# One core, eight images: row gathers without accumulation, row statistics moved to GpSimd, and sorting, scatters and logits spread over more steps

## The chip, the cores and the metric

The kernel runs on one core of one Trainium2 chip. The metric is the device time of one execution in microseconds (us). Engines: PE is TensorE (matrix products; PEld its weight loads), DVE is VectorE, ACT is ScalarE, POOL is GpSimd, SP is SyncE, which here only issues transfers. Each engine runs its own list of instructions in order and waits on semaphores where it needs another engine's result.

## What is computed

Eight images of 48x48 positions with 128 channels each. Per image:

```
x = x + ss2d(group_norm(x))            # 32 groups; 256 inner channels, 3x3 depthwise convolution,
                                       # scan over L = 2304 positions with 16 states:
                                       #   h = exp(dt*A)*h + dB*x ;  y = sum(h*C) + Dskip*x
t = tokens(x)                          # 2304 rows of 128
t = t + attention(layer_norm(t))       # 8 heads of 16, linear attention: softmax(q), softmax(k),
                                       # context = k'v, out = q context, projection, layer_norm
u = layer_norm(t)                      # routing: logits = u Wg (8 experts), best two, softmax of the two
t = t + sum over the two experts of weight * W2 (silu(W1 u) * (W3 u + b3))
```

The first layer norm of the tokens is followed at once by the one that the attention applies, so a row needs three statistics (a mean and a variance over 128 channels): of the tokens (two norms folded into one), of the attention's output, and of the sum.

## The kernel before

A row tile is 128 rows, so an image has 18 of them (NT). The scan takes an image in 6 chunks (c) of 384 positions; a chunk has 32 steps (n), one for each block of 8 of the 256 inner channels with 16 states on 128 partitions. A pass has 192 steps (k = 32c + n). All engines walk the same steps, and the images are pipelined over passes: in a pass one image is scanned (i), the image before it goes through attention, routing and scatter (j), the one before that through its experts (p), the one before that has its results gathered and summed (q), and the next image is loaded, normalised and convolved (nx). L420 and the lines behind it write the passes out: eight with a scan, of which images 3 to 6 are a loop; then a last pass without a scan (T_END = 362 steps), in which image 7 is routed, image 6's and image 7's experts run, and the last results are gathered.

In each step of the scan PE spreads the inputs (L768) into one of three PSUM buffers, DVE multiplies (inflow, L1407) and scans (L1420), ACT makes the decay three steps ahead (L1041), POOL multiplies the state by C (prod, L627, eight buffers) and PE folds that (L831). Around it:

- **Row statistics** (DVE): `spread_of` (L1497 to L1504), eight operations on 128x18 numbers, each waiting for the one before by a semaphore (`tie`); ACT takes the root (L1161, L1163); `offsets` (L1507). At steps 22, 24, 26 (T_STAT, with L1594 to L1599), 82 and 84 (T_STAT2), 98 and 100 (T_STAT3).
- **Routing**: the logits (PE, L896, 18 products, six a step from step 110), best two (DVE, from 113), the rank by a product at 118, sorting into expert tiles at 119 to 123.
- **Scatter** (POOL, L681): 36 indirect DMAs that write rows of 129 numbers to `rows_in` in DRAM, one at each step from 125 to 160; after 18 of them the weight column is replaced (L678).
- **Experts**: 45 tiles of 128 rows, some at steps 126 to 191 and the rest at steps 0 to 26 of the pass behind. A tile is loaded, transposed (PE L910, ACT L1209), multiplied up (PE L921 and L933, ACT L1212 and L1221, DVE L1661), its two halves multiplied on POOL (`hidden`, L697), multiplied down (PE L940), and stored to `rows_out`.
- **Gather** (POOL, L709): 36 indirect DMAs per image with compute_op=ADD; SP first loads a row tile of the sum so far into one of six buffers (acc_in, L573), each gather adds 128 rows of 128 numbers to it, the second one 4 steps behind the first, which it waits for; SP stores the tile as output (L577). Steps 34 to 110 of a pass.
- **The next image**: x_in has three buffers of a sixth of an image; its loads are issued at steps 114 to 116, and from step 128 on behind the transposes (PE L738) that free a buffer. Transposes at 125 to 135, statistics of each sixth (L1366), group norm (L1371 to L1378 at step 138, L1382 to L1385 at 140, L1389 at 141) and the normalising at step 145.
- **Products with weights on POOL**: L663, L668 (attention output, steps 86 to 94), L656 (62 to 64), L633 and L640 once a chunk.

Of the kernel before, what the change touches and what calls it, by code (L numbers as in the profile page):

```python
# [47 lines left out]
XR, XI = 2, 3  # L48
WA, WB = 3, 5
UIN, UOUT, UT, HID = 7, 3, 3, 2  # L50
GA = 6
# [12 lines left out]
T_XLOAD = tuple(NB * TURN - 14 + g if g < XI else T_TURN[g - XI] + 3 for g in range(NC))  # L64
# [5 lines left out]
T_STAT, T_BACK, T_NORM = 22, 25, 29  # L70
# [17 lines left out]
T_END = T_GATHER[-1] + STORE + 1 + SC - SOONEST  # L88
DVE_POST = 53
# [3 lines left out]
LAG = 2  # L93
TILE = tuple(T_TILE + (T_LAST - T_TILE) * u // (NU + LAG - 1) for u in range(NU + LAG))

# [54 lines left out]
def build(nc, a):  # L150

    with ExitStack() as ctx:
# [3 lines left out]
        def psum(name):  # L156
# [27 lines left out]
        x_in = sb("x_in", [P, XI, TT, D])  # L184
# [27 lines left out]
        acc_in = sb("acc_in", [P, GA, D])  # L212
# [3 lines left out]
        gdev = sb("gdev", [P, 2 * NC])  # L216
# [13 lines left out]
                             for k in range(3))  # L230
        tile_expert, expert_of = sb("tile_expert", [P, NU]), sb("expert_of", [P, 2, NU], I32)
# [6 lines left out]
        acc = q_tok  # L238
# [116 lines left out]
        s_x = [Sem(f"s_x{b}", NC // XI, 16) for b in range(XI)]  # L355
# [4 lines left out]
        dve_gn = Sem("dve_gn", NC + 9)  # L360
# [21 lines left out]
        s_weight, s_rows = Sem("s_weight", 1), Sem("s_rows", 1)  # L382
        s_accout = Sem("s_accout", 1, 16)
        s_top, s_topexp, s_sorted = Sem("s_top", 1), Sem("s_topexp", 1), Sem("s_sorted", 2)
        dve_post = Sem("dve_post", DVE_POST)
# [9 lines left out]
        s_gather = [Sem(f"s_gather{b}", NT // GA * TOP, 16) for b in range(GA)]  # L395
        s_accin = [Sem(f"s_accin{b}", NT // GA, 16) for b in range(GA)]
        s_out = [Sem(f"s_out{b}", NT // GA, 16, first=16) for b in range(GA)]

# [34 lines left out]
        def _(sp):  # L433
# [69 lines left out]
            def load_x(w, g):  # L503
                if w.nx is None:
                    return
                if g >= XI:
                    sp.wait_ge(*full(w.nx, f"xT{g - XI}"))
                elif w.i is not None:
                    sp.wait_ge(*full(w.i, f"xT{g + NC - XI}"))
                apart()  # L510
                sp.dma_start(x_in[:, g % XI], x_chunk(w.nx, g)).then_inc(s_x[g % XI].sem, 16)
# [38 lines left out]
            def experts(m, t):  # L550
# [15 lines left out]
                for x in range(NT):  # L566
                    if t == T_GATHER[x] - 3:
                        if x == 0:
                            due(sp, s_accout, m, 1)
                            apart()  # L570
                        due(sp, s_out[x % GA], m, x // GA)
                        apart()
                        sp.dma_start(acc_in[:, x % GA], image_rows(acc_dram, m)[:, D * x:D * x + D]).then_inc(s_accin[x % GA].sem, 16)  # L573
                    if t == T_GATHER[x] + STORE:
                        due(sp, s_gather[x % GA], m, TOP * (x // GA + 1))
                        apart()
                        sp.dma_start(a["out"][bass.ds(image_of(m), 1)][:, P * x:P * x + P, :].rearrange("o p d -> p (o d)"),  # L577
                                     acc_in[:, x % GA]).then_inc(s_out[x % GA].sem, 16)

            def run(w, first, last):  # L580
                for k in range(first, last):
# [11 lines left out]
                    for g in range(NC):  # L593
                        if k == T_XLOAD[g]:
                            load_x(w, g)
# [13 lines left out]
            for b in range(GA):  # L609
                sp.wait_ge(s_out[b].sem, s_out[b].at(B, 0))  # L610

        @block.gpsimd
        def _(pool):
# [28 lines left out]
            def attention(m, t):  # L642
                if m is None:
                    return
                for h in range(2):
# [23 lines left out]
                k = t - T_SCATTER  # L669
                if 0 <= k < NSC:  # L670
# [13 lines left out]
            def experts(m, t):  # L684
                if m is None:
                    return
                if t == T_ROWS:
                    for b in range(GA):
                        due(pool, s_gather[b], m, s_gather[b].per)
                    pool.sem_inc(s_rows.sem, 1)  # L690
# [7 lines left out]
                for n in range(TOP):  # L698
                    if t - SECOND * n in T_GATHER:
                        x = T_GATHER.index(t - SECOND * n)  # L700
                        if n == 0:
                            if x == 0:
                                for b in range(UOUT):
                                    due(pool, s_ostore[b], m, s_ostore[b].per)
                            due(pool, s_accin[x % GA], m, x // GA + 1)
                        else:
                            due(pool, s_gather[x % GA], m, TOP * (x // GA) + 1)
                        pool.sem_inc(s_sp.sem, 1)
                        pool.indirect_dma_start(acc_in[:, x % GA], None, rows_out,  # L709
                                                bass.IndirectOffsetOnAxis(ap=row_of[:, parity(m), n * NT + x:n * NT + x + 1], axis=0),  # L710
                                                compute_op=ALU.add).then_inc(s_gather[x % GA].sem, 16)

            def run(w, first, last):
                for k in range(first, last):
# [8 lines left out]
                    attention(w.j, k)  # L723
# [282 lines left out]
        def _(act):  # L1006
# [225 lines left out]
            def attention(m, t):  # L1232
                if m is None:
                    return
                if t == T_STAT + 1:
                    root(m, 1, r1[:, :])
# [497 lines left out]
```

## Time and profile before

| | us |
|---|---|
| time, median of 3 runs | 4248.45 (4237.47 to 4254.57) |
| the profiled execution | 4259.8, of which the span is 4257.7 |
| PE busy | 3281.3 (77%) |
| DVE busy | 3117.9 (73%) |
| POOL busy | 2942.6 (69%) |
| ACT busy | 2565.0 (60%) |
| mean granted clock of PE | 0.89 of full speed |

By the start of their first scan the passes take 361, 401, 444, 489, 491, 502, 489 and 469 us (images 0 to 7), behind a start of 86 us, and the last pass 526 us. Times are read from one profiled execution. The busy share is an average over stages that have different limits, so the stretches of one pass are what is read below; a stretch is a chunk of 32 steps or a part of it. A row of the windows gives from:to and its length, then the busy time and number of instructions of PE, PEld, DVE, ACT and POOL in that order, then the granted clock of PE, the DMA share and GB/s; the stretch of chunk 2 begins at step 62. A bracket behind an operation is the idle time of its engine before it and what ended it.

### The profile page before, as it was taken

What the parts mean: (1) busy time and instruction counts of PE and PEld (TensorE: products, weight loads), DVE (VectorE), ACT (ScalarE), POOL (GpSimd) and SP (SyncE); (2) the same over time, 40 slices, a digit from 0 to 9 for tenths busy, and PEclk for the clock granted to TensorE, in tenths of its full rate; (3) what the DMA queues carried; (4) which work ended last, traced back from release to release, by engine and by line L of the source; (5) the groups of instructions that cost most, each with busy time, mean ns of one, the idle gap of its engine ahead of it and who ended that gap; (6) DMA issues with size and microseconds to landing.
All of it is one profiled execution on the core that took longest, in us unless ns stands there. A gap on an engine that the chain in (4) does not pass through costs nothing.

```text
span 4257.7 us, 69497 instructions
## 1 busy us (share of the span) xinstructions
PE 3281.3 (77%) x17432; PEld 1995.0 (47%) x17432; DVE 3117.9 (73%) x5570; ACT 2565.0 (60%) x6151; POOL 2942.6 (69%) x2703
## 2 busy tenths in 40 slices
PE   5687887787798868987788877888688877778381
PEld 2233343343465535653465434655356534567271
DVE  3699998899867987789776988779877897723110
ACT  3465665476567656775576755676467765666151
POOL 1465675857676968679685886669686796757665
PEclk9798997898899979998899978999799988999695
DMA  4865555555787658966687676876588666868493
GB/s 103 194 154 134 145 127 124 135 144 139 189 218 201 144 142 218 235 164 145 169 226 193 146 164 177 219 195 143 140 228 233 154 149 178 221 184 231 117 257 76
DMA packets 464099, 730.07 MB, mean 171 GB/s; under 512 B 58505, under 2 KB 362194, under 8 KB 461522
## 3 DMA queue, kind: packets, MB, share of 16 engines
q1 hardware_dynamic: 313938, 484.13, 46.5%
q10 hardware_dynamic: 99072, 203.47, 16.1%
q0 software_dynamic: 50688, 37.93, 5.2%
q8 instruction: 152, 2.49, 0.3%
q14 instruction: 249, 2.04, 0.2%
HBM read 596.93 MB, written 100.07 MB: 164 GB/s over the span
## 4 chain that ended last, share of the span: by engine, by line
PE 34%; issue 17%; DVE 16%; POOL 14%; ACT 11%; DMA 4%; ACTq 2%; SPq 1%; DVEq 0%; POOLq 0%
PE ps_conv L754 7%; DVE state L1420 6%; PE ps_main L817 5%; POOL prod L627 5%; PE ps_h L921 3%; PE ps_y L831 3%; POOL rows_in L681 3%; PE ps_g L940 3%; DVE ps_x L1407 3%; PE ps_x L768 3%; PE ps_g L933 3%; POOL acc_in L709 3%; ACT dt_rep L1041 2%; ACT big_u L1169 1%; DVE silu L1661 1%
## 5 line engine op out<-in xcount | busy, mean ns | idle before, releaser
L627 POOL TENSOR_TENSOR prod<-state,c_rep 128x384 f32<-128x384 f32 x1536 | 1659.0, 1120 | 937.9 <-DVE state L1420 912.9
L1420 DVE TENSOR_TENSOR_SCAN state<-dt_rep,carry,ps_x 128x384 f32<-128x384 f32 x1280 | 1284.0, 1003 | 0.0
L1407 DVE TENSOR_TENSOR ps_x<-ps_x,db_rep 128x384 f32<-128x384 f32 x1536 | 854.0, 556 | 397.7 <-PE ps_x L768 360.0
L1041 ACT ACTIVATE dt_rep<-dt_rep,vecs 128x384 f32<-128x384 f32 x1536 | 913.3, 611 | 182.0 <-DMA dt_rep<-dt_dram 104.1
L768 PE MATMUL ps_x<-x_stack,copy 96*128 96x384 bf16 x1536 | 546.9, 357 | 392.3 <-DVE state L1420 386.4
L754 PE MATMUL ps_conv<-gx,w_conv 128*128 128x384 f32 x1728 | 695.9, 522 | 8.7 <-DVE parts L1437 6.0
L768 PEld LDWEIGHTS ps_x<-x_stack,copy 96*128 96x128 bf16 x1536 | 154.5, 101 | 882.1 <-DVE state L1420 635.9
L709 POOL DMA_INDIRECT acc_in<-rows_out,row_of x288 | 452.6, 1572 | 97.8 <-issue 46.3
L921 PE MATMUL ps_h<-u_t,w_up 128*128 128x128 f32 x2064 | 325.1, 296 | 188.4 <-DVE silu L1661 170.5
L697 POOL TENSOR_TENSOR hidden<-g_sb,silu 128x384 f32<-128x384 f32 x344 | 363.7, 1060 | 104.4 <-ACT u_out L1227 98.9
L754 PEld LDWEIGHTS ps_conv<-gx,w_conv 128*128 128x128 f32 x1728 | 320.9, 203 | 227.6 <-issue 119.7
L1221 ACT ACTIVATE g_sb<-ps_g,w_down 128x128 f32<-128x128 f32 x1032 | 304.1, 368 | 199.6 <-PE ps_g L940 164.6
L1661 DVE SCALAR_TENSOR_TENSOR silu<-silu,ps_h 128x384 f32<-128x384 f32 x344 | 185.8, 540 | 300.4 <-ACT silu L1212 193.6
L921 PEld LDWEIGHTS ps_h<-u_t,w_up 128*128 128x128 f32 x2064 | 275.5, 200 | 276.2 <-issue 165.9
L831 PE MATMUL ps_y<-prod,fold 128*32 128x384 f32 x3072 | 361.2, 545 | 22.9 <-POOL prod L627 22.9
L681 POOL DMA_INDIRECT rows_in<-big_u,row_of x288 | 291.1, 1011 | 83.8 <-issue 76.4
L940 PE MATMUL ps_g<-w_down,hidden 128*128 128x128 f32 x2064 | 299.4, 282 | 34.1 <-POOL hidden L697 25.4
L933 PE MATMUL ps_g<-u_t,w_up 128*128 128x128 f32 x2064 | 309.4, 288 | 11.9 <-ACT u_out L1227 8.1
L933 PEld LDWEIGHTS ps_g<-u_t,w_up 128*128 128x128 f32 x2064 | 289.3, 202 | 51.4 <-issue 25.9
L940 PEld LDWEIGHTS ps_g<-w_down,hidden 128*128 128x128 f32 x2064 | 268.2, 198 | 41.7 <-POOL hidden L697 29.0
L1420 DVE TENSOR_TENSOR_SCAN state<-dt_rep,ps_x 128x384 f32<-128x384 f32 x256 | 241.4, 943 | 16.4 <-ACT carry L1050 16.4
L1212 ACT ACTIVATE silu<-ps_h 128x384 f32<-128x384 f32 x344 | 168.1, 489 | 48.6 <-POOL hidden L697 38.6
(245 smaller groups left out, 4928.9 us busy)
## 6 DMA issues: line engine op xcount, KB each, us to landing
dt_rep<-dt_dram SPq DMA_DIRECT2D x384, 768.0 KB
w_up<-in_w_exp ACTq DMA_DIRECT2D x344, 384.0 KB
w_down<-in_w_exp ACTq DMA_DIRECT2D x344, 193.5 KB
x_stack<-parts SPq DMA_DIRECT2D x576, 48.0 KB
u_in<-rows_in SPq DMA_DIRECT2D x344, 64.5 KB
rows_out<-u_out SPq DMA_DIRECT2D x344, 64.0 KB
dt_dram<-dt SPq DMA_DIRECT2D x192, 96.0 KB
x_in<-in_x SPq DMA_DIRECT2D x48, 192.0 KB
```

The lines of the kernel that those rows point to most:

```text
L627: pool.tensor_tensor(prod[:, k % HS, :], state[:, k % HS, :], c_rep[:, c % 2, :], ALU.mult).then_inc(s_prod.sem, 1)
L681: pool.indirect_dma_start(rows_in, bass.IndirectOffsetOnAxis(ap=row_of[:, parity(m), k:k + 1], axis=0), big_u[:, k % NT, :], None).then_in ...
L709: pool.indirect_dma_start(acc_in[:, x % GA], None, rows_out, bass.IndirectOffsetOnAxis(ap=row_of[:, parity(m), n * NT + x:n * NT + x + 1], ...
L754: ins = pe.matmul(aux(use)[:, 0:T], w_conv[:, tap, P * hf:P * hf + P], gx[:, ROWS * c + dy:ROWS * c + dy + ROWS, dx:dx + W], start=tap == ...
L768: pe.matmul(ps_x[k % XB][:, 0:T], copy[:, b, :], x_stack[:, c % 2, HV * q + hf, :], start=True, stop=True).then_inc(s_xrep.sem, 1)
L831: ins = pe.matmul(ps_y[32 * q:32 * q + 32, 0:T], fold[:, b, :], prod[:, (QD * m + q) % HS, :], start=b == 0, stop=b == 3)
L921: ins = pe.matmul(aux(name)[:, P * k:P * k + P], w_up[:, u % WA, P * k:P * k + P], u_t[:, u % UT, :], start=True, stop=True)
L933: ins = pe.matmul(aux(name)[:, P * k:P * k + P], w_up[:, u % WA, F + P * k:F + P * k + P], u_t[:, u % UT, :], start=True, stop=True)
L940: ins = pe.matmul(aux(name)[:, F:F + P], hidden[:, v % HID, P * k:P * k + P], w_down[:, v % WB, P * k:P * k + P], start=k == 0, stop=k == ...
L1041: act.activation(dt_rep[:, g % XS, q, :], dt_rep[:, g % XS, q, :], ACT.Exp, scale=decay_rate).then_inc(s_decay.sem, 1)
L1407: dve.tensor_tensor(x_n, x_n, db_rep[:, c % 2, :], ALU.mult).then_inc(s_inflow.sem, 1)
L1420: dve.tensor_tensor_scan(state[:, k % HS, :], dt_rep[:, g % XS, q, :], ps_x[k % XB][:, 0:T], init, ALU.mult, ALU.add).then_inc(s_state.sem, 1)
```

## The change

In neutral words, part by part:

1. **Gather**: 36 plain gathers (no compute_op) into `got` (two pairs of row tiles, two rows each), at T_GATHER = 34 + 23x//5 (steps 34 to 112), the second two steps behind the first, and none waits for another. POOL adds: at T_SUM (43, 52, 62, 71, 80, 89, 98, 108, 117) a 128x256 addition of the two gathers, a step later a 128x256 addition to acc_in, which SP loads and stores by pairs.
2. **Row statistics**: `spread_of` and `offsets` run on POOL (26 small operations an image, 19 of which are followed by a wait for themselves, `settle`), at steps 23, 25, 27 / 82, 84 / 97, 99. ACT's root takes the scale and the small constant.
3. **Group norm**: one bn_aggr in place of L1371 to L1378, at n = 9 in place of 10; three of the small operations go to ACT.
4. **Next image**: x_in lies where the sum (`acc`, q_tok) lay; six loads issued at steps 112 to 117, and the first transpose waits for all.
5. **Logits and sorting**: six steps of three products (108 to 113) in place of three of six; best two from 114, rank at 121 and copied by ACT, sorting at 122 to 130.
6. **Scatter**: steps 132 to 190, spread (132 + 58k//35); for the last image 132 + k. T_END is 368.

The core of the diff:

```diff
-T_XLOAD = tuple(NB * TURN - 14 + g if g < XI else T_TURN[g - XI] + 3 for g in range(NC))
+T_XLOAD = NB * TURN - 16
-T_STAT, T_BACK, T_NORM = 22, 25, 29
+T_STAT, T_BACK, T_NORM = 23, 25, 29
-T_AGAIN, T_STAT2, T_NORM2, T_STAT3, T_NORM3, T_UT, T_LOGIT = 81, 82, 85, 98, 101, 103, 110
+T_AGAIN, T_STAT2, T_NORM2, T_STAT3, T_NORM3, T_UT, T_LOGIT = 81, 82, 85, 97, 100, 102, 108
-T_TOP, T_RANK, T_SORT, T_SCATTER = 113, 118, 119, 125
+T_TOP, T_RANK, T_SORT = 114, 121, 122
-T_GATHER = tuple(2 * SC + k for k in (34, 37, 40, 43, 46, 49, 52, 66, 69, 72, 75, 78, 81, 84, 97, 100, 103, 106))
-T_ROWS, SECOND, STORE = 2 * SC + 114, 4, 9
+T_GATHER = tuple(2 * SC + 34 + 23 * x // 5 for x in range(NT))
+SECOND = 2
+T_SUM = tuple(T_GATHER[2 * g + 1] + SECOND + 3 for g in range(NG))
+STORE = 4
+T_SCATTER = tuple(132 + 58 * k // (NSC - 1) for k in range(NSC))
+T_SCATTER_LAST = tuple(132 + k for k in range(NSC))
...
-        acc = q_tok
+        acc = x_in = q_tok
...
+            def settle(m, ins):
+                count[0] += 1
+                ins.then_inc(pool_post.sem, 1)
+                due(pool, pool_post, m, count[0])
+
+            def spread_of(m, src):
+                settle(m, pool.tensor_tensor(mv[:, :, 0], src[:, :, 1], src[:, :, 4], ALU.subtract))
+                settle(m, pool.tensor_tensor(mv[:, :, 1], src[:, :, 2], src[:, :, 5], ALU.add))
+                settle(m, pool.tensor_tensor(mv[:, :, 0], mv[:, :, 0], mv[:, :, 0], ALU.mult))
+                pool.sem_inc(s_sp.sem, 1)
+                settle(m, pool.tensor_scalar(mv[:, :, 0], mv[:, :, 0], D / 4.0, None, ALU.mult))
+                pool.tensor_tensor(mv[:, :, 1], mv[:, :, 0], mv[:, :, 1], ALU.add).then_inc(s_var.sem, 1)
+
+            def offsets(m, src):
+                settle(m, pool.tensor_tensor(mv[:, :, 0], src[:, :, 1], src[:, :, 4], ALU.add))
+                pool.sem_inc(s_sp.sem, 1)
+                settle(m, pool.tensor_scalar(mv[:, :, 0], mv[:, :, 0], -0.5, None, ALU.mult))
+                pool.tensor_tensor(nb[:, :], mv[:, :, 0], r1[:, :], ALU.mult).then_inc(s_coef.sem, 1)
...
+                if t in (T_STAT2, T_STAT3):
+                    due(pool, s_stats, m, 1 if t == T_STAT2 else 2)
+                    spread_of(m, st)
+                if t in (T_STAT2 + 2, T_STAT3 + 2):
+                    due(pool, s_root, m, 3 if t == T_STAT2 + 2 else 4)
+                    offsets(m, st)
...
-                        pool.indirect_dma_start(acc_in[:, x % GA], None, rows_out,
-                                                bass.IndirectOffsetOnAxis(ap=row_of[:, parity(m), n * NT + x:n * NT + x + 1], axis=0),
-                                                compute_op=ALU.add).then_inc(s_gather[x % GA].sem, 16)
+                        pool.indirect_dma_start(got[:, g % RG, n, x % 2, :], None, rows_out,
+                                                bass.IndirectOffsetOnAxis(ap=row_of[:, parity(m), n * NT + x:n * NT + x + 1], axis=0)
+                                                ).then_inc(s_gather[g % RG].sem, 16)
+                for g in range(NG):
+                    first = got[:, g % RG, 0]
+                    if t == T_SUM[g]:
+                        due(pool, s_gather[g % RG], m, 2 * TOP * (g // RG + 1))
+                        pool.tensor_tensor(first, first, got[:, g % RG, 1], ALU.add).then_inc(s_sum.sem, 1)
+                    if t == T_SUM[g] + 1:
+                        due(pool, s_sum, m, 2 * g + 1)
+                        due(pool, s_accin[g % RG], m, g // RG + 1)
+                        pool.tensor_tensor(acc_in[:, g % RG], acc_in[:, g % RG], first, ALU.add).then_inc(s_sum.sem, 1)
...
-                due(pe, s_x[g % XI], i, g // XI + 1)
+                due(pe, s_x, i, NC)
...
+                if n == 9:
+                    dve.sem_inc(s_sp.sem, 1)
+                    dve.bn_aggr(gmv[:, 0:2], gst[:, :, :].rearrange("p g k -> p (g k)")).then_inc(s_gn.sem, 1)
```

## Rows read from the trace of the kernel before

**Rows 1.** The page's first part: busy time of each engine, share of the span

```profile
PE 3281.3 (77%) x17432; PEld 1995.0 (47%) x17432; DVE 3117.9 (73%) x5570; ACT 2565.0 (60%) x6151; POOL 2942.6 (69%) x2703
```

**Rows 2.** Windows of image 4 (chunks 0, 2, 4, 5): us, busy by engine, clock, DMA

```profile
1781.30:1860.40 79.10, 68.22 (x407) 44.48 (x406) 61.24 (x106) 61.07 (x152) 46.81 (x47) 0.96 0.77 203
...
1929.00:2004.80 75.80, 55.84 (x258) 28.01 (x251) 71.62 (x128) 43.26 (x97) 72.11 (x63) 0.84 0.63 142
...
2092.00:2187.00 95.00, 79.26 (x482) 56.06 (x481) 68.85 (x115) 63.00 (x164) 79.30 (x79) 0.94 0.81 221
2187.00:2272.40 85.40, 75.78 (x482) 53.02 (x481) 60.94 (x96) 58.07 (x156) 57.06 (x57) 0.98 0.86 229
```

**Rows 3.** Timeline of DVE, image 4, step 22: start, duration, operation

```profile
1840.46 0.17 DVE L1497 TENSOR_TENSOR mv<-st_t 128x18 f32<-128x18 f32 x1
...
1843.62 0.57 DVE L1407 TENSOR_TENSOR ps_x<-ps_x,db_rep 128x384 f32<-128x384 f32 x1
```

**Rows 4.** Timeline of all engines, image 4, around step 82

```profile
1966.25 3.43 DVE L1497 TENSOR_TENSOR mv<-st 128x18 f32<-128x18 f32 x1
...
1970.15 3.22 DVE L1500 SCALAR_TENSOR_TENSOR mv<-mv 128x18 f32<-128x18 f32 x1
1970.79 2.54 POOL L627 TENSOR_TENSOR prod<-state,c_rep 128x384 f32<-128x384 f32 x2
...
1976.25 0.57 DVE L1407 TENSOR_TENSOR ps_x<-ps_x,db_rep 128x384 f32<-128x384 f32 x1
1976.36 0.22 ACT L1161 ACTIVATE r<-r 128x18 f32<-128x18 f32 x1 [12.58 <-DVE r L1504]
```

**Rows 5.** POOL by line, image 4, steps 62 to 95: busy, mean ns, idle before

```profile
L627 POOL TENSOR_TENSOR prod<-state,c_rep 128x384 f32<-128x384 f32 x33 | 43.8, 1441 | 2.9 <-DVE state L1420 2.9
L709 POOL DMA_INDIRECT acc_in<-rows_out,row_of x14 | 22.0, 1572 | 2.2 <-issue 1.9
```

**Rows 6.** Durations by line, whole trace: ns least/median/most, first and last start

```profile
L681 POOL DMA_INDIRECT rows_in<-big_u,row_of x288: 959/998/1719, 718.4 to 4021.8; - x144
L709 POOL DMA_INDIRECT acc_in<-rows_out,row_of x288: 1542/1571/1624, 1378.6 to 4252.3; - x144
L678 POOL COPY big_u<-gw x8: 205/210/218, 762.9 to 3981.9; 128x18 f32<-128x18 f32 x8
L633 POOL TENSOR_TENSOR dt<-dt,dt_tmp x48: 1792/1818/2412, 71.6 to 3605.7; 128x768 f32<-128x768 f32 x48
```

**Rows 7.** Timeline of POOL, image 4, the scatter behind L678

```profile
2144.54 1.71 POOL L681 DMA_INDIRECT rows_in<-big_u,row_of  x1 [0.89 <-POOL big_u L678]
```

**Rows 8.** Timeline of DVE, image 4, step 98

```profile
2010.17 0.17 DVE L1497 TENSOR_TENSOR mv<-st 128x18 f32<-128x18 f32 x1
...
2013.77 0.57 DVE L1407 TENSOR_TENSOR ps_x<-ps_x,db_rep 128x384 f32<-128x384 f32 x1
```

**Rows 9.** PE by line, image 4, steps 110 to 114: busy, mean ns, idle before

```profile
L896 PE MATMUL ps_g<-w_gate,qv 128*128 128x8 f32 x36 | 6.3, 308 | 1.4 <-ACT qv L1032 1.4
```

**Rows 10.** Timeline of PE, image 4, step 135

```profile
2115.79 0.52 PE L738 MATMUL ps_conv<-eye,x_in 128*128 128x128 f32 x3 [3.43 <-DMA x_in<-in_x]
```

**Rows 11.** Timeline of DVE, image 4, steps 138 to 141

```profile
2121.72 0.14 DVE L1371 TENSOR_REDUCE gmv<-gst 128x1 f32<-128x12 f32 x1
...
2124.78 0.56 DVE L1661 SCALAR_TENSOR_TENSOR silu<-silu,ps_h 128x384 f32<-128x384 f32 x1
...
2135.91 0.16 DVE L1389 TENSOR_SCALAR gmv<-ps_conv 128x1 f32<-128x1 f32 x1 [2.65 <-PE ps_conv L745]
```

**Rows 12.** Waits in chunk 4 of image 7 (89.4 us): total, times, longest

```profile
ACT silu L1212 <- POOL hidden L697: 11.8, 5, 5.6
```

**Rows 13.** Timeline of POOL, the last gathers

```profile
4175.37 1.58 POOL L709 DMA_INDIRECT acc_in<-rows_out,row_of  x1 [5.11 <-DMA acc_in<-acc_dram]
4177.25 1.56 POOL L709 DMA_INDIRECT acc_in<-rows_out,row_of  x1 [0.30 <-issue]
...
4252.27 1.56 POOL L709 DMA_INDIRECT acc_in<-rows_out,row_of  x1 [0.70 <-issue]
```

More of the change, by code:

```diff
@@ L352, in build @@
         s_sp = Sem("s_sp", 0)
-        s_x = [Sem(f"s_x{b}", NC // XI, 16) for b in range(XI)]
+        s_x = Sem("s_x", NC, 16)
         s_res = [Sem(f"s_res{b}", NC // XR, 16) for b in range(XR)]
@@ L505, in load_x @@
                     return
-                if g >= XI:
-                    sp.wait_ge(*full(w.nx, f"xT{g - XI}"))
+                if g:
+                    pass
+                elif w.j is not None:
+                    due(sp, s_accout, w.j, 1)
+                    apart()
+                    due(sp, s_xn, w.j, 3 * NC)
                 elif w.i is not None:
-                    sp.wait_ge(*full(w.i, f"xT{g + NC - XI}"))
+                    sp.wait_ge(*full(w.i, f"xT{NC - 1}"))
                 apart()
-                sp.dma_start(x_in[:, g % XI], x_chunk(w.nx, g)).then_inc(s_x[g % XI].sem, 16)
+                sp.dma_start(x_in[:, TT * g:TT * g + TT], x_chunk(w.nx, g)).then_inc(s_x.sem, 16)
             def load_residual(w, c):
@@ L592, in run @@
                         store_t1(w, c)
-                    for g in range(NC):
-                        if k == T_XLOAD[g]:
-                            load_x(w, g)
+                    if 0 <= k - T_XLOAD < NC:
+                        load_x(w, k - T_XLOAD)
                     for m, t in w.experts(k):
@@ L608, in _ @@
             passes(sp, run)
-            for b in range(GA):
+            for b in range(RG):
                 sp.wait_ge(s_out[b].sem, s_out[b].at(B, 0))
@@ L686, in experts @@
                     return
[L687 to L690, printed above, removed]
                 u = tile_of.get(t - 3)
@@ L894, in logits @@
                         pe.wait_ge(*read(m, x))
-                for k in range(6 * part, 6 * part + 6):
+                for k in range(TT * part, TT * part + TT):
                     ins = pe.matmul(o[:, NE * k:NE * k + NE], turned[:, P * k:P * k + P], w_gate[:, :], start=True, stop=True)
-                if part == 2:
+                if part == NC - 1:
                     ins.then_inc(fills("logit", m), 1)
@@ L1552, in count_experts @@
             def count_experts(m):
-                dve.wait_ge(*full(m, "rank"))
-                tie(m, dve.tensor_copy(tally[:, 0, :], aux("rank", m)[:, NE * NT:NE * NT + NE]))
-                tie(m, dve.tensor_scalar(tally[:, 3, :], tally[:, 0, :], 1.0 / P, None, ALU.mult))
+                dve.wait_ge(*read(m, "rank"))
+                tie(m, dve.tensor_scalar(tally[:, 3, :], counts[:, NE * NT:NE * NT + NE], 1.0 / P, None, ALU.mult))
                 tie(m, dve.tensor_tensor(picked[:, :, :], tally[:, 3, :].unsqueeze(2).broadcast_to([P, NE, NT]),
```

242 lines of the change are left out of this document (111 added, 131 removed).

## The prediction

> **What bounds the kernel now.** I read first the page's busy times [rows 1]: PE 77%, DVE 73%, POOL 69%, and nobody is full. Such a page says that the loss is in the coupling, so the next view is the windows of one pass, chunk by chunk [rows 2], of image 4, since images 3 to 6 run the same loop. There each chunk has another limit. Chunk 0 takes 79.1 us with PE busy for 68.2 and POOL for 46.8: PE is near its end, POOL has 32 us free. From step 62 to 95 (75.8 us) it is POOL with 72.1, and DVE shows 71.6. Chunk 4 takes 95.0 with PE and POOL both at 79.3; chunk 5 85.4 with PE at 75.8 and POOL at 57.1. Then I read the timelines where steps are long. The scan needs PE's spread, DVE and POOL in turn with only a few buffers between, so whatever holds DVE for some us in one step is mostly lost to the pass, even where DVE has idle time a few steps later.
>
> Four such places stand out. At step 22 the eight row statistics hold DVE from 1840.46 to 1843.62, 3.2 us [rows 3]. At step 82 the same eight hold it from 1966.25 to 1976.25, 10 us [rows 4]: an operation on 18 numbers that takes 0.17 alone lasts 3.4 or 3.2, and the 3.22 us one ends with POOL's two multiplications that run beside it. ACT waits 12.58 us for the result. At step 98 they take 3.6 us [rows 8]. And at step 138 the group norm's eight take 3.1 [rows 11], a few steps behind PE's wait of 3.43 for x_in [rows 10].
>
> **The change part by part.** The sum is made against the profiled 4259.8; it is 11.4 above the median of 4248.45, and I subtract the difference from the median.
>
> *Statistics.* DVE loses 30 small operations an image, POOL gets 26. What one costs on POOL: its 128x18 copy takes 0.21 [rows 6]. Its wait for itself has no row; the scatter behind the copy, which waits in that way, starts 0.89 us later [rows 7], where a DMA without such a wait starts 0.30 behind the one before it [rows 13], so at most 0.6. From the other side, eight operations linked in the same way on DVE take 3.1 us with all waits [rows 11], under 0.4 each. I take 0.32 for operation and wait, nearer to the second row since both are chains of computation. Steps 23 to 27 on POOL: 10 x 0.32 = 3 us, hidden in its 32 free us. DVE's 3.2 us at step 22 go, and five more operations at 24 and 26 of at least 0.17 each: 4 us, all counted (bounds -1, if PE with 68.2 of 79.1 is late next, to -5). At step 98 it is 3.6, counted as 3.3, in a chunk where POOL has room.
>
> At step 82 POOL has none, and this is the place where I don't count what DVE loses. POOL's account for steps 62 to 95 [rows 5, 6]: 14 accumulating gathers of 1.57 with 0.16 of issue, 24.2 us, go. 15 plain ones come. No plain gather is in the trace; the nearest is the scatter, also an indirect DMA of 128 rows without an accumulation, 1.00 us; with 0.16 that makes 17.4. Bounds are 1.00 and 1.57, and I take the lower. Four sum pairs lie here. From 1.82 for 768 columns and 0.21 for 18 a 256-column addition is 0.21 + 238 x 2.14 ns = 0.72; with two waits a pair is 1.56, four are 6.2. The statistic at 82 and 84 is eight operations, 2.6. Together -24.2 + 17.4 + 6.2 + 2.6 = +2.0. So the stretch stays as long as it is, though DVE is rid of 10 us: DVE waits for POOL where it now waits inside its own operations. Bounds -7 (sums and statistics find gaps) to +12 (each own wait 0.6, and the sums wait for late gathers).
>
> A rule of the Trainium skill speaks against this move: "GPSIMD Engine Reference", section 4.1, keeps elementwise work of two inputs on VectorE, with GpSimd about half as fast. By it an operation would be about 0.36 us and the sum here some 1 us per statistic later; the copy's 0.21 against 0.17 on DVE doesn't show a factor of two at 18 columns [rows 3, 6].
>
> *Logits.* PE's products of 8 columns take 6.3 us in three steps (the row counts 36) and hold the spread of steps 112 and 113 behind them [rows 9]; three a step instead of six is counted as -2. Sorting keeps its DVE work, in nine steps for five: 0, and at worst +2 where a step with sorting meets a full one of POOL. Chunk 3 with step 98: -5.3, say -5.5.
>
> *Next image.* The loads are issued at 112 to 117 rather than up to step 132, so the wait of 3.43 [rows 10] goes: -3 (the six in a burst delay other loads at worst by 2). They need the sum's last reader, long done at step 112. Behind them on SP stand the decay loads and the tiles' row loads, both some steps early.
>
> *Group norm.* bn_aggr for eight operations: 3.1 less one of at most 0.6, since 384 columns take 0.57 [rows 3, 11], -2.5. Of the small ones at 140 and 141 DVE keeps two; its wait of 2.65 for PE there goes, as ACT takes that step, and three operations of 0.2 to 0.4: -3.5. Bounds -2 to -6.
>
> *Scatters.* They leave steps 125 to 131 and lie at 132 to 190, 17 in chunk 4 and 19 in chunk 5 (35 and 1 before). An issue costs 1.00 + 0.25. Chunk 5's POOL goes from 57.1 to 57.1 + 18 x 1.25 = 79.6 of 85.4. I count +2 there and -0.5 in chunk 4, which with x_in and group norm gives -9.5.
>
> Images 3 to 6: -4 + 0 + 2 - 5.5 - 9.5 + 2 = -15 each, -60 (chunk 1 has none of the edits that count). Image 7 has no next image: -4 + 2 - 5.5 - 3.5 (35 scatters spread where POOL makes ACT wait 11.8 us [rows 12]) = -11. Image 2, with no gathers in its pass, -16.5; image 1, in its short chunks, -13; image 0 has only the group norm, -5; the start -1.5.
>
> *The last pass.* Its end is POOL alone, from 5.11 before 4175.37 to 4257.7, 87.4 us: 36 gathers 1.88 apart and four waits of 5 for acc_dram [rows 13]. After: a pair of tiles is 4 x 1.28 + 1.95 = 7.07, nine are 64, with 7 for the first landing and the last store 71: -16 (bounds 0 at 1.57 a gather, to -20). The two earlier gather phases of this pass and image 7's scatters: -14 (bounds 0 to -25).
>
> Sum: -1.5 - 5 - 13 - 16.5 - 60 - 11 - 30 = -137. 4259.8 - 137 - 11.4 = 4111.
>
> **The rivals.** *A, the plain gather costs 1.57 too* (issue time is per row, not per kind). For it: both move 128 rows. Against: the scatter's 1.00. Then +0.57 x 15 = 8.6 in five passes and 36 x 0.57 = 20.5 in the end: 4111 + 63 = 4174.
>
> *B, PE takes what DVE gives back.* For it: 68.2 of 79.1 and 79.3 of 95.0 [rows 2]. Against: PE waits for DVE's scan in these steps. Chunks 0, 3 and 4 give 3, 4 and 5 less in six passes: +72, 4183.
>
> *C, slower: POOL's statistics hold ACT.* A statistic becomes a chain POOL, ACT, POOL, ACT, in POOL's order behind its multiplications. It decides where POOL lags the scan by more than the three steps by which ACT's decay is early; then ACT, which waits in order, starves the scan. The price is what ACT waits at step 82, 12.58 [rows 4], at the two other places too, in seven passes: 2 x 12.6 x 7 = 176, 4287. Against it: POOL has 32 us free in chunk 0, so it doesn't lag there.
>
> *D, more is gained: POOL yields at step 82.* DVE's 10 us go there whole and the +2 with them, in five passes: 4111 - 60 = 4051. For it: DVE's waits there end with POOL's operations, so it is DVE that yields now. The Trainium skill, "SBUF — State Buffer", section on the two sides, says that DVE and GpSimd hold a shared port pair exclusively for a whole instruction; the 3.22 us ending with POOL's multiplications agrees [rows 4], and by that rule the blocked time leaves with the moved operations.
>
> *E, scatters in chunk 5 make POOL late.* Above 85.4 - 79.6 = 5.8 us of waits POOL becomes the bound and `hidden` comes late, as image 7's chunk 4 shows [rows 12]. Price 18 x 1.25 = 22.5 less the 2 counted, in seven passes: +143, 4254, no change.
>
> **How the numbers follow.** Forecast 4111: 0.42, its own range 4075 to 4150. A 0.12, B 0.12, C 0.10, D 0.15, E 0.09. A measurement of this kernel tells about 0.5% from no change, 21 us, so faster means under 4227: forecast, A, B and D, 0.81; same is E, 0.09; slower C, 0.10. The range leaves out C and E (0.19): from below D, 4020, to above B with its bounds, 4215.
>
> **What would show it.** In the changed kernel's windows: chunk 0 near 75, steps 62 to 95 near 76 with POOL still above 70, chunk 4 near 85, chunk 5 near 87. On the gather's line near 1.00 us; a POOL operation of 18 columns near 0.21 with gaps near 0.1. PE's transposes of x_in without a wait for DMA. The end from the last tile on near 71. Wrong would make it: gathers at 1.57 (A), ACT waiting for POOL's r or nb for over 7 us in chunk 0 or 3 (C), waits for `hidden` over 10 us in chunk 5 (E), or DVE without a wait for POOL at step 82 (D).

## The result: 0.7% faster, a fifth of what was forecast

The changed kernel takes 4227.05 us (median of 18 runs, 4209.72 to 4244.81) against 4254.66 for the kernel before in the same sessions (18 runs): a ratio of 0.9931, 95% interval 0.9916 to 0.9945. It is faster, as forecast, by 28 us and not by 137; the time lies above the range. The profiled execution went from a span of 4257.7 to 4218.1, -39.6, 12 us more than the medians differ by, and the readings below are made against that pair.

| where (profiled spans, us) | forecast | measured |
|---|---|---|
| start | -1.5 | +1.1 |
| image 0 | -5 | -5.8 |
| image 1 | -13 | -13.4 |
| images 2 to 6, five passes | -76.5 | +22.9 |
| image 7 | -11 | -12.6 |
| last pass | -30 | -31.8 |

The miss is in the five passes that have both expert tiles and a next image. For one of them, by stretches of steps (mean of images 2 to 6; the forecast is that for images 3 to 6):

| steps | what the change does there | forecast | measured |
|---|---|---|---|
| 0 to 31 | first statistic | -4 | -2.9 |
| 32 to 61 | gathers, sums | 0 | -0.2 |
| 62 to 96 | gathers, sums, second statistic | +2 | 0.0 |
| 97 to 107 | third statistic | -3.5 | +2.4 |
| 108 to 113 | logits | -2 | -1.6 |
| 114 to 131 | sorting | 0 | +4.1 |
| 132 to 144 | next image, group norm | -9 | -5.1 |
| 145 to 149 | (normalising, no edit counted) | 0 | +5.6 |
| 150 to 164 | scatters | -0.5 | -1.3 |
| 165 | (weight copy, no edit counted) | 0 | +4.7 |
| 166 to 191 | scatters | +2 | -1.0 |
| all | | -15 | +4.6 |

The windows of image 4 in the changed kernel, which answer to [rows 2] (chunk 0, steps 62 to 95, chunks 4 and 5; columns as there):

```profile
1772.40:1850.40 78.00, 68.23 (x406) 44.18 (x405) 56.95 (x93) 58.27 (x148) 49.48 (x58) 0.95 0.79 207
...
1918.30:1995.80 77.50, 54.87 (x260) 26.34 (x252) 62.06 (x120) 43.18 (x97) 71.07 (x79) 0.87 0.57 141
...
2084.10:2181.10 97.00, 79.68 (x474) 55.74 (x475) 71.71 (x111) 61.29 (x160) 66.53 (x65) 0.91 0.75 199
2181.10:2268.40 87.30, 76.02 (x482) 52.69 (x481) 60.94 (x96) 57.50 (x156) 70.55 (x72) 0.98 0.88 235
```

DVE is rid of 4.3 us in chunk 0 and of 9.6 from step 62 to 95, and POOL of 12.8 in chunk 4. Yet chunk 4 is longer (97.0 against 95.0), with DVE 2.9 us busier. Durations of POOL's operations, which answer to [rows 6] (least, median and most in ns):

```profile
L756 POOL DMA_INDIRECT got<-rows_out,row_of x288: 940/987/1052, 1367.4 to 4211.7; - x144
...
L763 POOL TENSOR_TENSOR got<-got x72: 717/730/750, 1389.4 to 4214.3; 128x256 f32<-128x256 f32 x72
...
L663 POOL TENSOR_TENSOR mv<-st x16: 235/244/254, 599.2 to 3889.4; 128x18 f32<-128x18 f32 x16
```

A plain gather takes 0.99 us where an accumulating one took 1.57, an addition of 256 columns 0.73, a small operation 0.24, or 0.35 from its start to that of the next behind its wait, where 0.32 was forecast: the prices were right. The last gathers, which answer to [rows 13]:

```profile
4153.65 0.99 POOL L756 DMA_INDIRECT got<-rows_out,row_of  x1 [4.01 <-DMA rows_out<-u_out]
4154.94 0.94 POOL L756 DMA_INDIRECT got<-rows_out,row_of  x1 [0.30 <-issue]
...
4214.27 0.72 POOL L763 TENSOR_TENSOR got<-got 128x256 f32<-128x256 f32 x1 [1.61 <-DMA got<-rows_out,row_of]
```

From the wait ahead of the first (4149.6) to the end (4218.1) the phase takes 68.5 us, 87.4 before; 71 was forecast.

### The profile page after: what moved, and what is told of

Same layout as the page of the kernel before. It is cut to its first block and busy times, and to the rows that moved or that the text cites. A ratio compares the mean times of both kernels' runs of the same rounds, so it can differ in the third digit from the quotient of the medians.

```text
span 4218.1 us, 69032 instructions
## 1 busy us (share of the span) xinstructions
PE 3292.7 (78%) x17432; PEld 1992.9 (47%) x17432; DVE 3006.8 (71%) x5234; ACT 2556.1 (61%) x6173; POOL 2917.0 (69%) x3055
## 3 DMA queue, kind: packets, MB, share of 16 engines
q10 hardware_dynamic: 99072, 203.47, 16.1%
## 5 line engine op out<-in xcount | busy, mean ns | idle before, releaser
L638 POOL TENSOR_TENSOR prod<-state,c_rep 128x384 f32<-128x384 f32 x1536 | 1530.2, 1002 | 899.3 <-DVE state L1471 867.5
L745 POOL TENSOR_TENSOR hidden<-g_sb,silu 128x384 f32<-128x384 f32 x344 | 343.6, 999 | 115.0 <-ACT u_out L1291 103.4
L756 POOL DMA_INDIRECT got<-rows_out,row_of x288 | 283.9, 986 | 61.9 <-issue 38.7
L996 PEld LDWEIGHTS ps_g<-w_down,hidden 128*128 128x128 f32 x2064 | 268.3, 198 | 41.5 <-POOL hidden L745 31.5
L1273 ACT ACTIVATE u_t<-ps_h 128x128 f32<-128x128 f32 x328 | 89.8, 274 | 195.9 <-PE ps_h L966 179.3
```

The source lines that it names most:

```text
L638: pool.tensor_tensor(prod[:, k % HS, :], state[:, k % HS, :], c_rep[:, c % 2, :], ALU.mult).then_inc(s_prod.sem, 1)
L745: pool.tensor_tensor(hidden[:, u % HID, :], g_sb[:, u % 2, :], silu[:, u % 2, :], ALU.mult).then_inc(s_hidden.sem, 1)
L996: ins = pe.matmul(aux(name)[:, F:F + P], hidden[:, v % HID, P * k:P * k + P], w_down[:, v % WB, P * k:P * k + P], start=k == 0, stop=k == ...
```

## The experiments

Times are medians; each kernel is the changed one with one edit, and "after" is the changed kernel. Five-pass means are of images 3 to 7 unless it is said otherwise. The kernel before took 4250.8 to 4257.9 us by the median beside these runs, so their times can be set against the changed kernel's 4227 to within some 10 us.

**The weight copy.** What was read first, in image 4 of the changed kernel around step 165 (timeline; in brackets the idle time before and what ended it):

```profile
2192.19 0.21 POOL L730 COPY big_u<-gw 128x18 f32<-128x18 f32 x1 [5.64 <-DMA rows_in<-big_u,row_of]
...
2196.23 0.49 ACT L1276 ACTIVATE silu<-ps_h 128x384 f32<-128x384 f32 x1 [4.08 <-POOL hidden L745]
...
2200.32 0.57 DVE L1458 TENSOR_TENSOR ps_x<-ps_x,db_rep 128x384 f32<-128x384 f32 x1 [3.01 <-PE ps_x L824]
```

POOL stands still for 5.64 us until the eighteenth scatter has landed, `hidden` is late, so ACT is late, so the spread. Ahead of the copy stands one operation of 1.00 us behind the scatter's issue (2184.51 to 2185.52). Before the change, in image 4, there were three, and no wait:

```profile
2138.73 1.00 POOL L681 DMA_INDIRECT rows_in<-big_u,row_of  x1 [0.16 <-issue]
2139.77 1.00 POOL L627 TENSOR_TENSOR prod<-state,c_rep 128x384 f32<-128x384 f32 x1
2140.72 1.81 POOL L640 TENSOR_TENSOR y<-y,sz 128x768 f32<-128x768 f32 x1
2142.50 0.99 POOL L697 TENSOR_TENSOR hidden<-g_sb,silu 128x384 f32<-128x384 f32 x1
2143.44 0.21 POOL L678 COPY big_u<-gw 128x18 f32<-128x18 f32 x1
```

```diff
-T_SCATTER = tuple(132 + 58 * k // (NSC - 1) for k in range(NSC))
+T_SCATTER = tuple(132 + 23 * k // (NT - 1) for k in range(NT)) + tuple(163 + 27 * k // (NT - 1) for k in range(NT))
```

> The changed kernel, but the first 18 scatters of an image lie at steps 132 to 155 and the other 18 at 163 to 190, so that the copy of the second weight column, which waits for the first 18 to land, comes eight steps behind the last of them and not one. Theory W (the wait behind the 18th scatter): in the changed kernel GpSimd stands 5.64 us before that copy at step 161, hidden comes late and step 165 lasts 7.5 us in place of 2.8; with the steps between, step 165 falls by about 4.7 us in six passes: 4227 - 28 = 4199 us. Rival E of the prediction (scatters in the last chunk are simply too much for GpSimd): the last chunk still has 18 of them, so it stays at 87 us and the time at 4227.

Measured: 4184.89 us, 0.9815 of the kernel before (0.9775 to 0.9855). Step 165 went from 7.2 to 2.6 us; the copy waits for no DMA anywhere in the trace, here in image 4:

```profile
2184.99 0.22 POOL L730 COPY big_u<-gw 128x18 f32<-128x18 f32 x1
```

The theory held for the step, but only about half of its gain reaches the time: steps 166 to 178 went from 28.9 to 31.4 us in images 2 to 6, and to 31.2 to 31.5 in the three kernels below that have this edit too. In image 3 ACT now waits there 2.7 us for a store of `rows_out`, which it doesn't in the changed kernel; whether waits of this kind make up the whole 2.5 us was not followed. Chunk 5 takes 82.1 us in images 2 to 6, 84.2 after and 81.9 before the change. So rival E of the prediction fell: with 18 scatters the chunk is as long as with one. The gain is nevertheless larger than expected because step 145 fell too, by 3.1 us in images 2 to 6 (5.2 with the steps up to 149), without an edit there; the third run tells why.

**Sorting.**

```diff
                 if t == T_SORT + 1:
                     count_experts(m)
+                    sum_experts(m)
                 if t == T_SORT + 2:
-                    sum_experts(m)
+                    place_experts(m)
+                    route(m, 7)
                 if t == T_SORT + 3:
-                    place_experts(m)
+                    place_rows(m, 0)
+                    place_rows(m, 1)
                 if t == T_SORT + 4:
-                    route(m, 7)
-                if t in (T_SORT + 5, T_SORT + 6):
-                    place_rows(m, t - T_SORT - 5)
-                if t == T_SORT + 7:
                     place_tiles(m, before_m)
-                if t == T_SORT + 8:
                     place_last(m)
```

> The changed kernel, but the sorting operations stand in five steps (122 to 126) and not in nine (122 to 130). Theory P (small VectorE operations stretched by GpSimd's multiplication, which starts anew in each step): VectorE's busy time of steps 114 to 131, 50.2 us in image 4 against 45.7 before the change, comes back to about 46 to 47, 3 to 4 us in each of seven passes: 4227 - 25 = 4202. Rival (the sum of the operations is the same wherever they stand, and TensorE's expert tiles set the pace of steps 126 to 131): no change, 4227.

Measured: 4232.1 us, 0.995 (0.9926 to 0.9975). The windows of steps 114 to 131 in image 4, first after, then this run:

```profile
2043.30:2096.40 53.10, 35.97 (x164) 19.53 (x165) 50.22 (x135) 18.60 (x46) 21.85 (x23) 0.78 0.48 124
```

```profile
2044.30:2098.90 54.60, 36.45 (x161) 19.86 (x162) 47.91 (x135) 18.67 (x46) 22.15 (x23) 0.78 0.48 124
```

DVE's busy time, the third number, fell by 2.3 us: the same operations last longer when they are spread. That POOL's multiplication stretches them was argued, not tried. In images 3 to 7 the time didn't follow (54.0 us, 52.7 after), as the rival says. In image 1, in whose pass there are no expert tiles, it did: 47.8 us, 49.7 after.

**Normalising the next image.** In image 4 of the changed kernel, step 145:

```profile
2133.16 4.58 DVE L1446 TENSOR_SCALAR gx<-gx,gmv 128x2304 f32<-128x2304 f32 x1
2133.62 1.95 POOL L638 TENSOR_TENSOR prod<-state,c_rep 128x384 f32<-128x384 f32 x2
2135.52 0.99 POOL L745 TENSOR_TENSOR hidden<-g_sb,silu 128x384 f32<-128x384 f32 x1
2136.69 1.94 POOL L733 DMA_INDIRECT rows_in<-big_u,row_of  x1 [0.17 <-issue]
```

```diff
+                    act.activation(inner, inner, ACT.Identity, bias=gmv[:, 6:7], scale=rate).then_inc(s_norm.sem, 1)
...
-                    dve.tensor_copy(gmv[:, 4:5], aux("gm")[:, 0:1])
+                    dve.tensor_scalar(gmv[:, 4:5], aux("gm")[:, 0:1], -1.0, None, ALU.mult)
...
-                    dve.tensor_scalar(inner, inner, gmv[:, 5:6], gmv[:, 6:7], ALU.mult, ALU.subtract).then_inc(s_norm.sem, 1)
```

> The changed kernel, but ACT and not VectorE multiplies the 2304 columns of the normalised next image (step 145). Theory P: VectorE's operation takes 4.58 us there because it stands behind two multiplications and a hidden of GpSimd (1.48 before the change, when GpSimd happened to issue a DMA); on ACT it meets no GpSimd operation: step 145 falls by 3 to 4.5 us in images 0 to 6, and steps 147 and 148, which were 2.7 longer at a granted clock of 0.79 (1.00 before), fall by up to 2.7 in images 2 to 6: 4227 - 20 to 4227 - 40, 4197 in the middle. Rival (ACT is late with the decay when it holds 2304 columns for 2 to 3 us): the gain is eaten, 4220 to 4230.

Measured: 4189.04 us, 0.9855 (0.9829 to 0.988). Step 145 fell by 4.5 us in images 2 to 6 and by 2 in images 0 and 1, steps 146 to 149 by about 1, to 15.5 (13.8 before). ACT's operation takes 2.3 us; the only wait for it is PE's of 3.9 us ahead of the first scan. The first run's DVE operation, with its durations over all images, and POOL's beside it in image 4:

```profile
L1446 DVE TENSOR_SCALAR gx<-gx,gmv x8: 1457/1458/1905, 35.2 to 3111.7; 128x2304 f32<-128x2304 f32 x8
...
2132.59 1.94 POOL L733 DMA_INDIRECT rows_in<-big_u,row_of  x1 [0.16 <-issue]
```

Before the change, in image 4, beside the scatter of [rows 7]:

```profile
2144.64 1.48 DVE L1395 TENSOR_SCALAR gx<-gx,gmv 128x2304 f32<-128x2304 f32 x1
```

In both the scatter steps put an indirect DMA on POOL just then (2132.59 to 2134.53 in the first run), and no multiplication until the operation was over. So the edit of the scatter, not one of the normalising, made this step long. The Trainium skill says in "SBUF — State Buffer", in the section on the two sides, that VectorE, in some kinds of operations, and GpSimd share a port pair, which one of them holds for a whole instruction while the other waits. The rows agree on the waiting: the operation ends at 2137.74, and 1.46 before that is 2136.28, near the end of POOL's third operation (2136.51). Why it waits past the ends of the first two is not shown.

**The statistics on DVE again.**

```diff
...
-                if t in (T_STAT2, T_STAT3):
-                    due(pool, s_stats, m, 1 if t == T_STAT2 else 2)
-                    spread_of(m, st)
...
+                if t in (T_STAT2, T_STAT3):
+                    due(dve, s_stats, m, 1 if t == T_STAT2 else 2)
+                    spread_of(m, st)
...
```

(and the first statistic and the offsets likewise)

> The changed kernel, but the three row statistics run on VectorE again, in the changed kernel's form and steps (part 2 undone alone). The prediction's theory (moving them gains 4 us in chunk 0 and 3.3 at the third, and costs 2.6 at the second): 4227 + 5 x 7 = 4260. Theory C' (a chain of GpSimd, ACT, GpSimd, ACT behind GpSimd's other work costs about what VectorE is rid of: step 82 gives 10 us back and steps 71 to 95 take 9 to 10 of it, step 98 gives 3.6 and steps 103 and 105 take 6.5): chunk 0 gets longer by 2, steps 97 to 107 shorter by 3 to 5, step 82 is 10 again: 4220 to 4235.

Measured: 4224.13 us, 0.9922 (0.9898 to 0.9946): the same as after. Steps 22 to 31 are 1.3 us longer, step 82 by 2.0 only, steps 83 to 96 shorter by 2.7, 97 to 107 by 0.9. The move of part 2 to another engine is worth nothing that the times can tell, as the second theory said, but two of its numbers were wrong: step 82 doesn't take 10 us again, and steps 97 to 107 give 0.9 and not 3 to 5. At step 82 there are now five small operations for eight, and POOL no longer has the accumulating gathers beside them; that this is the whole reason was argued, not tried. The 4260 of the first theory left its own 2.6 out: 4 and 3.3 less 2.6 are 4.7 a pass, which makes 4251, and that is missed too.

**Logits and sorting as before the change.**

```diff
-T_AGAIN, T_STAT2, T_NORM2, T_STAT3, T_NORM3, T_UT, T_LOGIT = 81, 82, 85, 97, 100, 102, 108
+T_AGAIN, T_STAT2, T_NORM2, T_STAT3, T_NORM3, T_UT, T_LOGIT = 81, 82, 85, 97, 100, 102, 109
-T_TOP, T_RANK, T_SORT = 114, 121, 122
+T_TOP, T_RANK, T_SORT = 112, 118, 119
```

(and three steps of six products, and the five sorting steps of the second run)

> The changed kernel, but part 5 undone: the logits in three steps of six products (109 to 111), best two from 112, rank at 118, sorting in five steps 119 to 123, as before the change but for one step. Theory T (what costs 4.1 us in steps 114 to 131 of each pass is that sorting now stands in steps 125 to 130, where the first expert tiles run and TensorE needs the step; the second run showed that fewer meetings with GpSimd alone don't give it back): these steps come back from 53.4 to about 49.5 us, 4 us in images 2 to 6 and 1 to 3 in 1 and 7: 4227 - 23 = 4204. The prediction's theory (spread logits gain 2 us, sorting is neutral): 4227 + 14 = 4241.

Measured: 4218.64 us, 0.9912 (0.9884 to 0.9941). Image 4, steps 108 to 113 and 114 to 131:

```profile
2021.30:2042.70 21.40, 19.99 (x70) 13.83 (x71) 12.44 (x36) 9.18 (x22) 14.23 (x14) 0.60 0.77 191
2042.70:2092.50 49.80, 31.73 (x156) 16.68 (x155) 45.12 (x115) 19.46 (x47) 22.25 (x23) 0.83 0.52 132
```

Steps 114 to 131 came back to 49.4 us (52.7 after), as expected; steps 108 to 113 went from 16.7 to 19.9. By the time, the two cancel but for 8 us, less than the medians can tell. So the late place of best two, rank and sorting costs 3 to 4 us a pass in steps 114 to 131, and the spread logits give back about as much (the last section says how far one profile can tell that). The run moves the three together and doesn't show which of them costs.

**The third statistic.** Image 4 of the changed kernel, steps 97 to 105:

```profile
1998.65 0.99 POOL L756 DMA_INDIRECT got<-rows_out,row_of  x1 [0.16 <-issue]
1999.66 1.96 POOL L638 TENSOR_TENSOR prod<-state,c_rep 128x384 f32<-128x384 f32 x2
2001.58 0.24 POOL L663 TENSOR_TENSOR mv<-st 128x18 f32<-128x18 f32 x1
...
2003.23 0.31 ACT L1223 ACTIVATE r<-mv,vecs 128x18 f32<-128x18 f32 x1 [4.55 <-POOL mv L668]
...
2009.01 1.26 ACT L1233 ACTIVATE big_u<-qv,nb,r 128x128 f32<-128x128 f32 x3 [3.28 <-POOL nb L674]
...
2010.42 0.52 PE L931 MATMUL ps_g<-eye,big_u 128*128 128x128 f32 x3 [2.84 <-ACT big_u L1233]
...
2019.92 0.57 DVE L1458 TENSOR_TENSOR ps_x<-ps_x,db_rep 128x384 f32<-128x384 f32 x1 [4.24 <-PE ps_x L824]
```

In steps 97 to 103 POOL starts its multiplication 2 to 7 us behind the start of the step's scan (1 to 2 us in steps 97 to 101 before the change), the statistic waits in its queue, ACT waits for the statistic, PE's transposes for ACT, and DVE's inflow for PE.

```diff
-T_GATHER = tuple(2 * SC + 34 + 23 * x // 5 for x in range(NT))
+T_GATHER = tuple(2 * SC + (34 + 23 * x // 5 if x < 12 else 106 + 3 * (x - 12)) for x in range(NT))
```

> The changed kernel, but the last six row tiles are gathered at steps 106 to 123 in place of 89 to 114, so that GpSimd has no gather and no sum between steps 90 and 105, where the third row statistic stands. Theory C' (GpSimd is up to 6.8 us behind the scan at steps 99 to 102, so ACT waits 4.6 us for the statistic and 3.3 for the offsets, and TensorE's transposes hold the spread): in images 3 to 7 steps 97 to 107 fall by 3 us, to what image 1 shows without gathers, and steps 83 to 96 by 3 to 5 as GpSimd has 6 fewer gathers there: 4227 - 30 = 4197. Rival (the chain itself is too long, one step earlier than before the change, whoever stands ahead of it): steps 97 to 107 stay, 4215 to 4227.

Measured: 4191.01 us, 0.9846 (0.9817 to 0.9874). Steps 83 to 96 went from 39.1 to 34.2 us, 97 to 107 from 26.6 to 22.4, and ACT's waits for POOL's statistic (for r) and offsets (nb) over the second and third statistic of image 4 are these (total, times, longest), first after, then in this run:

```profile
ACT r L1223 <- POOL mv L668: 15.8, 2, 11.3
...
ACT big_u L1233 <- POOL nb L674: 3.3, 1, 3.3
```

```profile
ACT r L1223 <- POOL mv L668: 10.3, 2, 7.8
...
ACT big_u L1233 <- POOL nb L674: 0.4, 1, 0.4
```

The theory held; the chain is not too long by itself. Steps 114 to 131, where some of the sums now stand, took 1.7 us more.

**Less work on POOL.**

```diff
-                        pool.tensor_tensor(k_tok[:, tiles, :], k_tok[:, tiles, :],
-                                           out_gamma[:, :].unsqueeze(1).broadcast_to([P, TT, D]), ALU.mult).then_inc(s_gam.sem, 1)
+                        part = k_tok[:, TT * g, 0:18]
+                        pool.tensor_tensor(part, part, out_gamma[:, 0:18], ALU.mult).then_inc(s_gam.sem, 1)
```

(and the additions of L720 cut likewise; the kernel leaves out the other columns)

> The changed kernel, but GpSimd's twelve products and sums of the attention's output (steps 86 to 95) take 18 columns in place of 384; the rest of those columns is left out. It asks what sets steps 71 to 96. Theory (GpSimd is the bound there, so VectorE's 10 us of step 82 came back as waits for GpSimd): 12 x 0.77 = 9 us less work, and steps 83 to 96 fall by 8 to 9 us in images 3 to 7, by about 3 in images 1 and 2, which have no gathers there. Rival (the chain over ACT and TensorE sets it): they fall by less than 3 us everywhere.

Measured: 4198.25 us in one execution, of which only the steps are read. Steps 83 to 96 fell from 39.1 to 35.0 us in the five passes with gathers, by about 0.5 in images 1 and 2. Image 4's steps 83 to 96, first after, then this run:

```profile
1957.70:1998.60 40.90, 22.50 (x77) 8.76 (x77) 27.13 (x56) 20.70 (x47) 38.26 (x47) 0.71 0.48 126
```

```profile
1963.50:1997.30 33.80, 18.93 (x73) 6.91 (x71) 26.60 (x57) 18.51 (x44) 29.69 (x48) 0.75 0.51 131
```

POOL's busy time, the fifth, is 38.26 of 40.90 and then 29.69 of 33.80. This lies between theory and rival: with gathers POOL is the bound there for a part, but of the 9 us that it is relieved of by the expectation 4.1 reach the time on the mean, 7.1 in image 4. What sets the rest isn't settled.

**Together.** These three kernels have the edits above and no others: the scatter's and the normalising's; these two and the moved gathers; these three and the statistics on DVE.

> The first and the third run together: scatters with eight steps between the two halves, and ACT normalises the next image. In the first run step 145 had fallen too (by 3.1 us, its operation 1.46 us, since other things stood on GpSimd there), so the two overlap in part: step 165 gives 28 us, steps 145 to 149 give 28 to 33: 4227 - 60 = 4167 us. If the two gains were the same one, the time would stay at the 4185 to 4189 of the single runs.

Measured: 4171.96 us, 0.9805 (0.9773 to 0.9837): the first and the third run's gains overlap in step 145 and add in the rest: 42 and 38 us less the 5.2 of steps 145 to 149 in five passes are 54, and 55 were measured.

> Three of the runs together: eight steps between the two halves of the scatter, ACT normalises the next image, and no gather between steps 90 and 105. If the three are independent places (steps 165, 145 to 149, 83 to 107), their gains add: 4172 for the first two, and about 10 us in each of five passes less 15 in all for the sums that now stand in the sorting: 4172 - 36 = 4136 us. If they are one slack that whoever comes first takes, the time stays near 4165.

Measured: 4145.4 us, 0.9753 (0.9727 to 0.9779). Step 165 is 2.6 us, steps 145 to 149 16.4 (20.7 after), 83 to 96 34.5. Three places that add up nearly as independent ones (4136 was expected), and a kernel 82 us faster than after by the medians.

> The same three, and the three row statistics on VectorE again. If the move of the statistics is worth nothing by itself (theory C'), this is within 0.5% of the run before it, about 4136 to 4145; the prediction's theory gives 5 x 7 = 35 us more, 4171.

Measured: 4144.47 us, 0.9745 (0.9717 to 0.9773). The place of the statistics makes no difference here either.

## Why the prediction was wrong

**What held.** That no engine bounds the kernel and that its stretches have to be read; the prices of the gather, the sum and the small operation; the start of the sum for chunk 0 (-2.9 for -4); POOL as the limit of steps 62 to 96, so that the 10 us of [rows 4] were not cashed (0.0 for +2); the last pass (-31.8 for -30); image 0 (-5.8 for -5). The wait of [rows 10] went: PE's transposes of x_in wait for no DMA. Rival A is out, with gathers at 0.99. Rival D's sign came, step 82 takes 1.9 us where it took 12.0, but not its gain: steps 83 to 96 went from 31.1 to 39.1. Rival B didn't show in chunk 0.

**What came out by luck.** Images 1 and 7 have the sums that were forecast (-13.4 for -13, -12.6 for -11) and not the terms. In image 1 steps 166 to 191 are 5.1 us longer, for which there was no term, and steps 108 to 113 are 6.3 shorter for 2. In image 7 step 165 is 5.3 us longer and steps 150 to 164 are 11.6 shorter, where the spread scatters were to give 3.5 in all.

**Slips that change little.** DVE loses 31 small operations and not 30; of the 35 scatters that the sum puts into chunk 4 before the change three stood in chunk 3; the price of a wait for oneself is 0.11 us in the statistics' term and 0.06 in that of the sums, which makes 0.4 in steps 62 to 95. The 0.21 of POOL's copy was set against the factor of two for operations with two inputs, but a copy has one; POOL's two-input operation took 0.24, 0.17 on DVE.

**The step that failed first: "in a chunk where POOL has room".** At step 98 I counted DVE's 3.3 us as gained because POOL is busy for 52.0 of chunk 3's 87.2 us. It has room in the chunk, not at that step: behind steps 62 to 95 it is late, and the statistic, being in its queue, is late with it. Steps 97 to 107 came to +2.4. This is rival C's mechanism at one of its places; its price was 4.55 and 3.28 us of ACT's waiting (together above the 7 that were named as its sign), not 12.6, and in chunk 0, where POOL has 32 us free, it didn't decide. The sixth run, which clears POOL's queue there, gets 4.2 us back.

**Second: sorting "0, and at worst +2".** It measured +4.1. I costed the sorting by its own operations, as if their place were free. In images 3 to 6 steps 126 to 131, into which most of it was moved, went from 13.5 to 18.4 us, while steps 119 to 125 gave only 2.9 back. The fifth run shows that the place costs (49.4 us when it is back). The first expert tiles run in the same steps, but they aren't needed for it: image 1 has none in its pass, and there these six steps went from 10.6 to 16.1, with PE waiting for DVE's scan. The second run gets DVE's stretched operations back and, where there are tiles, no time. How the two share the 4.1 stays open, and so do the 2.1 us of it that lie in steps 114 to 118.

**Third, and largest: two steps that no edit names.** The sum moved the scatters and costed their issue. It didn't ask what else their order on POOL decided. (a) The copy behind the eighteenth scatter waits for the scatter to land. Before, three operations of POOL (3.8 us) stood between the two, and it landed meanwhile, in image 4 at most 3.7 us behind its issue. In the changed kernel one of 1.00 us stands there, and the landing takes 6.7, with a DMA share of 1.00 in this time (0.94 before); POOL stood for 5.64 us, with `hidden` queued behind it: +4.7 in six passes. Which of the two lengthened the step by more, the missing operations or the slower landing, was not tried apart. [rows 7] showed the copy, and I took from it the price of a wait for oneself and not the wait for the DMA. (b) Before the change the normalising of the next image happened to run beside an indirect DMA; now it runs beside three elementwise operations: +5.6 with the steps behind it, in five passes. The first run gives both back, the third the second; but behind (a) steps 166 to 178 take 2.5 us of the 4.7 again, so the stall had covered something else, in image 3 a wait of ACT for a store. Rival E had the right victim (`hidden`) and the wrong cause: a wait, not the number of scatters.

**Fourth: next image and group norm, -5.1 for -9.** Steps 136, 138 and 141 gave 2.7, 3.1 and 2.5 us, as in the sum; step 142 took 2.6 back. There DVE waits for PE's spread, 2.74 us in image 3, behind a tile's products (`ps_g`) and those of `ps_main`, which PE makes without a gap: rival B, at this one step. No run was made on that.

By the ledger of one pass the first two make 10.0 of the 19.6 us between forecast and result, the third 10.3, the fourth 3.9, and smaller gains, above all of chunk 5 with -3, go the other way. That the statistics' move brings nothing (fourth and tenth run) I had half seen: the terms -4, +2 and -3.3 were to make -5, and are about 0.

## What to carry to other kernels

When an operation moves in an engine's queue, list what else that queue's order was covering: each wait in it that other operations ahead of it had hidden, and each other engine's operation that happened to meet a harmless neighbour. An engine with less to do ahead of a wait arrives early and shows it, and behind the first such wait there may be another. And room is to be read at the step, from how far the engine lags there, and not from the busy share of the chunk.

## What was not expected of the hardware

The same instructions of steps 108 to 113 take from 11.3 to 20.6 us, in one execution and from one execution to the next (28 passes of images 3 to 6 in seven kernels that have the same code in these steps). Two passes of the same loop in one execution of the changed kernel, images 3 and 4, steps 108 to 113:

```profile
1534.00:1547.90 13.90, 12.33 (x68) 8.36 (x67) 10.48 (x17) 7.98 (x19) 13.42 (x13) 0.88 0.66 187
2024.60:2043.30 18.70, 17.14 (x66) 11.30 (x66) 10.56 (x17) 9.94 (x22) 14.12 (x14) 0.63 0.82 222
```

and image 4 in the third run:

```profile
1999.40:2010.70 11.30, 10.12 (x65) 7.05 (x63) 10.22 (x16) 7.87 (x19) 10.95 (x11) 1.00 0.86 225
```

PE is busy for nearly the whole stretch in each, and its granted clock is 0.88, 0.63 and 1.00 of full speed: between its two levels of 1.2 and 2.4 GHz for a part of the stretch, or at the upper one throughout. Just ahead of it, in steps 97 to 107, PE waits for ACT in all three (rows of the third statistic); what decides between them is not shown. Five passes of up to 9 us either way are as large as the whole gain of this change, so a single profile of this kernel can't price an edit to these steps, and the -1.6 measured for the logits is within that. All together tell more: the 28 passes take 17.5 us on the mean, and eight passes with six products a step (images 3 to 6 of the kernel before and of the fifth run) 20.3, none under 19.0. By that the spread logits do give the 2 us that were forecast, or a little more.
